# The low halves of layer 1's first two weight chunks move from VectorE to GpSimd, and the last two update chunks are split in natural order

## What is computed

```python
# layer 0, the part that matters here
nf2 = jnp.concatenate([n_f, z_f], axis=1)          # node features and attention sums, 256 x 2048
h_new = jax.nn.relu(nf2[:64] @ W_hn + b_hn)        # the "update"
o_new = jax.nn.relu(nf2[64:] @ W_on + b_on)
x = _layernorm(x + concat([h_new, o_new]))         # called x1 in the kernel
# layer 1
h = x @ W                                          # W is 1024 x 1024, "l1" in the kernel
e = exp(-leaky_relu(al[src] + ar[dst], 0.1))       # al, ar: h times two vectors
h_prime = segment_sum(e * h[dst], src) / (rowsum + 1e-5)
x = _layernorm(x + elu(h_prime))
```

## Time and profile before

| | |
|---|---|
| median of 3 runs | 355.23 us (353.24, 355.23, 358.76) |
| the profiled execution, its time | 354.13 us |
| its span, first to last instruction | 352.1 us |
| mean granted TensorE clock over the span | 0.986 of full |
| busy, share of the span | TensorE 92%, VectorE 82%, ScalarE 55%, GpSimd 33% |
| DMA over the span | 63.10 MB, 179 GB/s |

### The profile page before, as it was taken

One profiled execution on the slowest core, in us unless ns is written; L12 is line 12 of the kernel. 1 busy time (PEld: TensorE's weight loads), 2 busy tenths in 40 slices (PEclk: granted clock), 3 DMA queues, 4 the chain that ended last, 5 costly groups with the idle time before them and its releaser, 6 DMA issues.

```text
span 352.1 us, 4667 instructions
## 1 busy us (share of the span) xinstructions
PE 322.8 (92%) x1462; PEld 250.6 (71%) x1462; DVE 290.5 (82%) x416; ACT 195.2 (55%) x304; POOL 116.4 (33%) x126
## 2 busy tenths in 40 slices
PE   2899999999999999799999999999899997979980
PEld 1768887776654788578888888888686776858730
DVE  0799999985789979699999999988879879873545
ACT  2755296222042343698888888636149566641245
POOL 4300043065000740069999999710002100060000
PEclk9999999999999999899999999999999999999996
DMA  7999499779998996002130000023597886000003
GB/s 229 398 406 366 161 311 403 268 259 230 285 362 287 372 377 230 2 0 76 46 121 0 2 1 3 0 61 119 178 353 292 314 306 229 0 2 1 0 0 119
DMA packets 17638, 63.10 MB, mean 179 GB/s; under 512 B 2234, under 2 KB 2236, under 8 KB 17360
## 3 DMA queue, kind: packets, MB, share of 16 engines
q1 hardware_dynamic: 13520, 50.07, 39.1%
q0 software_dynamic: 2096, 8.74, 8.3%
q10 hardware_dynamic: 2000, 4.00, 3.3%
HBM read 59.64 MB, written 3.16 MB: 178 GB/s over the span
## 4 chain that ended last, share of the span: by engine, by line
PE 44%; DVE 44%; ACT 5%; DMA 4%; issue 2%; SPq 0%; ACTq 0%; DVEq 0%
DVE ps L1013 24%; PE ps L1212 11%; PE ps L1256 8%; DVE W_lo L776 7%; PE ps L1467 6%; PE ps L1407 3%; PE ps L1231 3%; PE ps L1399 3%; DMA x_nat<-in_x_dram 2%; PE ps L1501 2%; PE ps L1432 2%; DMA W_raw<-in_L_gnn_W_dram 2%; DVE tile_val L796 1%; DVE lo_in_raw L776 1%; PE ps L1288 1%
## 5 line engine op out<-in xcount | busy, mean ns | idle before, releaser
L487 ACT CAST W_hi<-W_raw 128x1024 fp32r<-128x1024 f32 x62 | 63.2, 1045 | 54.0 <-DMA W_raw<-in_L_gnn_W_ho_dram 24.5
L1013 DVE SCALAR_TENSOR_TENSOR ps<-ps,wa_bc 128x1024 f32<-128x1024 f32 x73 | 86.4, 1265 | 2.8 <-PE ps L1365 2.8
L776 DVE TENSOR_TENSOR W_lo<-W_raw,W_hi 128x1024 fp32r<-128x1024 f32 x54 | 65.2, 1238 | 9.3 <-ACT W_hi L487 7.0
L1365 PE MATMUL ps<-A_tab,oh 128*128 x146 | 53.1, 445 | 2.4 <-ACT oh L593 2.4
L1212 PE MATMUL ps<-W_hi,xT_hi 128*128 128x512 f32 x112 | 46.5, 415 | 0.6 <-DVE W_lo L776 0.6
L1365 PE MATMUL ps<-B_tab,oh 128*128 x146 | 46.4, 399 | 0.0
L1212 PE MATMUL ps<-W_lo,xT_hi 128*128 128x512 f32 x112 | 44.2, 394 | 0.0
L1212 PE MATMUL ps<-W_hi,xT_lo 128*128 128x512 f32 x112 | 35.0, 394 | 0.0
L441 POOL TENSOR_SCALAR sc<-sc 128x256 f32<-128x256 f32 x37 | 32.7, 884 | 3.3
L439 POOL TENSOR_TENSOR sc<-irow,keys 128x256 f32<-128x256 f32 x37 | 23.8, 642 | 27.9 <-PE ps L1372 27.1
L1365 PEld LDWEIGHTS ps<-B_tab,oh 128*128 128x128 f32 x146 | 28.0, 192 | 5.3
(11 more groups left out here) (277 smaller groups left out, 576.6 us busy)
## 6 DMA issues: line engine op xcount, KB each, us to landing
W_raw<-in_L_gnn_W_oo_dram SPq DMA_DIRECT2D x8, 1024.0 KB, 9.9
W_raw<-in_L_gnn_W_ho_dram SPq DMA_DIRECT2D x8, 1024.0 KB, 5.2
W_raw<-in_L_gnn_W_hh_dram SPq DMA_DIRECT2D x8, 1024.0 KB, 8.6
W_raw<-in_L_gnn_W_hn_dram SPq DMA_DIRECT2D x8, 1024.0 KB, 5.2
W_raw<-in_L_gnn_W_on_dram SPq DMA_DIRECT2D x8, 1024.0 KB, 5.6
W_raw<-in_L_gnn_W_dram SPq DMA_DIRECT2D x4, 1024.0 KB, 5.5
key_rows<-key_rows_scratch POOLq DMA_DIRECT2D x1, 2304.0 KB, 14.0
table_scratch<-tabs ACTq DMA_DIRECT2D x2, 1024.0 KB, 6.6
```

What stands on the lines that cost most here:

```text
L487: sa.copy(halves(n)[0], W_raw[:, n // 2 % NS, n % 2, :]).then_inc(hi_made, 1)
L776: v.tensor_tensor(lo, W_raw[:, n // 2 % NS, n % 2, :], hi.bitcast(F32), ALU.subtract).then_inc(lo_made, 1)
L1013: v.scalar_tensor_tensor(acc, acc, 0.0, wa_bc[:], ALU.max, ALU.mult, accum_out=keys[:, t, 2:3]).then_inc(reduced, 1)
L1365: ins = mm(acc[:, n * 512:(n + 1) * 512], oh[:, t // 2 % 2, k, t % 2 * P:(t % 2 + 1) * P], tab[:].rearrange("p q d -> p (q d)")[:, n * 512 ...
```

## The change

`by_pool` takes in chunks 80 and 81: GpSimd makes their low halves, behind its negation of `bias_bc` and ahead of its wait for the transposed x1. VectorE's list of low halves loses the two and runs to 79 in order. ScalarE makes the high halves of 78 and 79 right behind 77, that of 80 behind the copy `q0_low`, and that of 81 behind `q1_low`, ahead of 82 and 83. The list `made` goes, since all are made in natural order.

```diff
         def by_pool(n):
-            return END["hoB"] <= n < UX
+            return END["hoB"] <= n < UX or END["upd"] <= n < END["upd"] + 2
...
-        made = list(range(END["upd"] - 2)) + [END["upd"] + i for i in (0, 1, -2, -1)] + list(range(END["upd"] + 2, END["h1"]))
...
-            return sum(split(m) for m in made[:made.index(n) + 1])
+            return sum(split(m) for m in range(n + 1))
...
-            return sum(split(m) and by_pool(m) == pool for m in made[:made.index(n) + 1])
+            return sum(split(m) and by_pool(m) == pool for m in range(n + 1))
...
             ga.tensor_scalar(bias_bc[:, 1, :], bias_bc[:, 1, :], -1.0, None, ALU.mult).then_inc(less_target, 1)
+            lows(END["upd"], END["upd"] + 2)
             pool.wait_ge(pe_step, pe_at("x1T1"))
...
-            highs(UX + 4, END["upd"] - NB - 2)
-            high(END["upd"])
-            high(END["upd"] + 1)
-            high(END["upd"] - 2)
-            high(END["upd"] - 1)
+            highs(UX + 4, END["upd"] - NB)
...
             act.wait_ge(chunk_used, END["hn"])
             sa.copy(y2[0:Q, 0, :], G0[Q:P, D:2 * D]).then_inc(act_step, 1)
+            high(END["upd"])
             act.wait_ge(pe_step, pe_at("q1"))
             sa.copy(y2[Q:P, 0, :], G1[0:Q, 0:D]).then_inc(act_step, 1)
+            high(END["upd"] + 1)
             high(END["upd"] + 2)
             high(END["upd"] + 3)
...
-            lows(UX + NB + 4, END["upd"] - 2)
-            lows(END["upd"], END["upd"] + 2)
-            lows(END["upd"] - 2, END["upd"])
+            lows(UX + NB + 4, END["upd"])
```

## The result

The changed kernel runs in 351.43 us (median of 20 runs, 350.35 to 354.10), the kernel before in 356.23 us (20 runs, 352.65 to 358.76). The ratio is 0.9895, 95% interval 0.9873 to 0.9918: 1.05% faster, 3.7 us, within the 2% of the forecast. Ratios and counts leave out runs over 1.5% above the fastest of their kernel: three of these twenty of the kernel before (358.25 us and more; its median without them is 355.23) and four of its 63 runs with a clock on record (359.21 us and more, mean clocks of 0.967 to 0.971). The time lies inside the range of 350.4 to 355.6. The mechanism is the one predicted; the gain is larger than the 2.6 us of the sum, and the experiments are about that difference.

The account below looks back on a forecast made before the run. It took TensorE's 2.48 us wait for chunk 78, caused by VectorE making 80 and 81 first, as the bound. Removing 2.66 us less 0.05 of delay left 2.6, other parts costing nothing: median 355.23 - 2.6 = 352.6 us, range 350.4 to 355.6.

Parts of the forecast that it names:

- Low halves 78 and 79: VectorE makes both right behind 77: 78 starts at 288.45, 79 is over at 290.80, 2.66 us earlier.
- TensorE: The 2.48 us wait for chunk 78 goes; second pass, transposes and chunk 80 all come 2.6 us earlier.
- Merges and `mean0`: On VectorE behind low half 79: first merge near 290.8, both merges 2.6 us earlier, no slowdown from GpSimd.
- rival 2: GpSimd's low halves hold VectorE's merges for 4.8 us: 1.8 us slower, median 357.0; 3 in 100.
- GpSimd: Its low halves 80 and 81 take 2.40 us each, ending 293.7 and 296.6, ahead of TensorE's need; no cost.
- The hold on low half 82: VectorE's low half 82 waits 0.5 us for GpSimd's 81, hidden by 0.7 us of room; cost 0.
- the row of the subtraction: VectorE's low half at 313.60 beside GpSimd's subtraction took 2.36 us, 1.13 more than 1.23; read as milder than exclusion.
- The sum: 2.6 us gained on the chain: profiled time 354.13 to 351.5 us, span 352.1 to 349.5.
- a risk to the changed kernel: Clock rival: the wait near 311 brings 1.2 GHz behind it, costing 1.7 us, leaving 0.9, median 354.3; 5 in 100.
- The median: Median of the three runs before, 355.23, less 2.6 us: 352.6 us.
- The range: 350.4 to 355.6 us, 80 in 100; leaves out only the slower rival at 357.0.
- three of the four rivals: Layer norm loses 1.7 us (9 in 100); change does nothing (3 in 100); clock loses 1.7 us (5 in 100).

Follow-up runs that it names:

- `pool_only`: Kernel before with GpSimd making low halves 80 and 81, ScalarE keeping its old order 77, 80, 81, 78, 79: 359.17 us, ratio 1.0132 to before.
- `late_81`: Changed kernel with GpSimd's low half of 81 held back until `mean0`, to run beside VectorE's low half of 82: 353.44 us, ratio 0.9948 to before.
- filled kernels: Eight filling matmuls in each TensorE idle time: before (142, 289.9, 314 us) 352.71 us, ratio 0.9897; changed (142, 310 us) 350.31 us, ratio 0.9829.
- B empty: Kernel before with eight filling matmuls at 142 us and at 314 us, none in the wait for chunk 78 at 289.9: 353.99 us, ratio 0.9936.

## Why the prediction was right, and where it was off

The profiled execution is 1.03 us earlier ahead of the change, so its times plus 1.03 are on the scale of the prediction.

- **Low halves 78 and 79.** Predicted to end at 290.80; 286.30 + 3.50 + 1.03 = 290.83. The high halves were there, as worked out.
- **TensorE.** Predicted second pass over at 297.6, transposes at 299.0, chunk 80 at 301.5; measured 297.55 (first filling matmul), 298.94, 301.46.
- **Merges and `mean0`.** Predicted `mean0` near 295.8; 294.77 + 1.03 = 295.80. Merges take 1.22 to 1.24 us beside GpSimd, as alone: rival 2 is out.
- **GpSimd.** Predicted 291.3 and 294.2 at 2.40 us; 291.27 and 294.28 at 2.40 and 2.41.
- **The hold on low half 82.** Predicted 0.5 us, hidden; 1.67 - 1.23 = 0.44 us, hidden: the inverse root comes at 297.70 on the scale of the prediction, just 2.6 us earlier than in the earlier trace rows. `pool_only` and `late_81` show the price without that cover. The rule of the Trainium skill (SBUF — State Buffer, Who interferes with whom), whole-instruction exclusion, fits `late_81` and `pool_only` to 0.2 us. I called the row of the subtraction milder, and it is, for a `tensor_scalar` on GpSimd; beside a `tensor_tensor` there the rule is right.
- **The sum.** Predicted 2.6 us on the chain. The stage gave 2.63 in the profiled pair, and 2.4 between filled kernels. The term was right to 0.2 us. It rests on the load of 80 and 81, which I took at its one profiled landing; other executions put the same term at 2.3 and at 3.4.
- **What was left out.** The measured gain is 3.7 us. The step that failed is that I costed the wait at 289.9 at its own length and put no price on the clock behind it. The clock has a price only as a risk to the changed kernel ("With the matmuls 2.6 us earlier the wait near 311 could fall so that the clock goes to 1.2 GHz behind it", 5 in 100), and the wait that goes is named only as an argument against that risk ("one idle time fewer"). Both halves were off. The wait near 311 does bring a stretch, in the profiled execution among others, and by their mean clock 27 of 32 runs of the changed kernel hold at least one somewhere ahead of the end. But that holds for the kernel before too, which has a third such place, the very wait that the change removes: 49 of its 59 runs hold at least one, and 44 have a mean clock under 0.984, the mark of two or more. With all places filled the kernel before gains 355.34 - 352.71 = 2.6 us (its median over the 59), the changed one 351.51 - 350.31 = 1.2. The difference, 1.4 us, and the 2.4 us of the chain make the 3.8 us between these medians. The split is a rough one: the runs come from three sets whose medians of the kernel before are 355.23, 355.27 and 356.53, and the filled kernels ran in the last of them alone. The direct measure of the place at 289.9 is the 1.3 us between the kernel before with B empty and with all filled. I had one profile at a clock of 0.986, with no stretch behind 289.9, and read 1.00 there as a property of the kernel, not of that execution.
- **The median.** 352.6 was predicted, 351.43 measured. The base was not the cause: the runs of before that the ratio uses have a median of 355.23, as the three had. The forecast was 1.2 us off because the gain was 3.8 us between these medians and not 2.6.
- **The range.** 353.24 - 2.6 is 350.64; the 350.4 that stands there takes 0.2 us more. A range that holds the spread of single runs and three of the four rivals says little by being hit. What bears the mechanism out is the steps above, each within 0.1 us.

## What to carry to other kernels

Look for an engine whose order puts tiles not needed for 10 us ahead of two that are needed at once; here two engines did so, and both had to be mended together. Move elementwise work to GpSimd under VectorE instructions with an operand in PSUM, and check both ends of the overlap; beside instructions with two operands in SBUF it cost VectorE up to 2.25 of the 2.41 us that GpSimd's `tensor_tensor` took. Get a weight chunk's load out from between two tiles that are needed at once: the wait behind it was 0, 0.3 and 1.0 us in different executions. An idle time of TensorE can cost more than its length: fill it with matmuls on a copy of the kernel, at all places together, and compare; and set two versions against each other at equal clock before explaining tenths of a microsecond.

## What the runs showed of the hardware that was not expected

- An idle time of TensorE of 2.1 us between dense matmuls is followed by matmuls 0.43 us apart instead of 0.23 in part of the executions: one was profiled, and by the mean clock it is 8 of 12 with that place alone empty and none of 6 when it held eight matmuls too.
- Fillers cost nothing measurable (all filled 352.71 us; before, its runs with a mean clock of 0.989 and more, 352.85) and narrow the spread: before 354.75 to 357.90 us, all filled 352.39 to 353.20.
- Two `tensor_tensor` of 128 x 1024 with all operands in SBUF, on VectorE (1.23 us) and GpSimd (2.40 us), take turns: 3.38 and 3.35 us when each meets the other, 3.48 when VectorE is second by 0.01 us. GpSimd is held as VectorE is. In each of the four overlaps where VectorE came second (two in `pool_only`, one in `late_81`, one in the changed kernel) it was held 0.15 us less than GpSimd's instruction still had to run.
